# Attention stage: single steps with scores two steps ahead, a fifth slot of probabilities, and another join of the late maxima

## What is computed

```python
def xattn(q, k, v, Wq, Wk, Wv, bv, Wo, bo):       # 16 heads of 32
    qh, kh, vh = heads(q @ Wq.T), heads(k @ Wk.T), heads(v @ Wv.T + bv)
    scores = einsum('bhsd,bhtd->bhst', qh, kh) / sqrt(32)
    mask = triu(ones((S, S)), k=0).at[0, 0].set(False)
    scores = where(mask, -inf, scores)            # strictly causal, query 0 sees key 0
    out = einsum('bhst,bhtd->bhsd', softmax(scores), vh)
    return merge(out) @ Wo.T + bo
x = x + xattn(layernorm(x), ctx, ctx, ...)
x = x + ffn(layernorm(x), controller, f1, bias, f2)   # experts pick tokens by maximum
```

## Time and profile before

| | |
|---|---|
| median of three runs | 1348.98 us (1346.82 to 1352.07) |
| profiled execution | 1353.44 us, span 1351.7 us |
| mean granted TensorE clock over the span | 0.930 |
| busy over the span | PE 89%, PEld 61%, DVE 66%, ACT 45%, POOL 43% |
| attention stage | 313 to 927 us of the span |

### The profile page before, as it was taken

How to read it: one execution, slowest core, us unless ns; L and a number is a source line. 1 busy time by engine, 2 the same in 40 slices (tenths; PEclk the granted TensorE clock), 3 DMA queues, 4 the chain that set the end, 5 groups by cost and what they waited for, 6 DMA issues and landing times. The chain is left out here.

```text
span 1351.7 us, 29427 instructions
## 1 busy us (share of the span) xinstructions
PE 1203.2 (89%) x11456; PEld 830.9 (61%) x11456; DVE 890.0 (66%) x2198; ACT 612.6 (45%) x1143; POOL 583.6 (43%) x799
## 2 busy tenths in 40 slices
PE   5999999976889999999999999993799988898773
PEld 4888888853445555555555555541588877875552
DVE  6555555525666877777777778740578865559994
ACT  3222222201545555556656566552244444366651
POOL 0000000003446767777666666674576734302333
PEclk9999999995999999999999999997799977678986
DMA  6665555549623455555554444203788955453344
GB/s 228 217 217 207 213 210 209 186 156 198 143 68 77 108 126 126 126 126 126 126 125 106 114 113 113 69 17 112 266 260 264 297 168 188 168 190 89 111 128 148
DMA packets 163885, 210.77 MB, mean 156 GB/s; under 512 B 8880, under 2 KB 96560, under 8 KB 162736
## 3 DMA queue, kind: packets, MB, share of 16 engines
q1 hardware_dynamic: 163760, 209.06, 53.3%
HBM read 131.17 MB, written 77.59 MB: 154 GB/s over the span
## 5 line engine op out<-in xcount | busy, mean ns | idle before, releaser
L718 ACT ACTIVATE p_t<-p_bank 128x512 f32<-128x512 f32 (+1 forms) x608 | 310.2, 589 | 222.9 <-PE p_bank L778 217.3
L759 PE MATMUL p_bank<-k_stack,q_stack 96*128 96x512 f32 (+3 forms) x768 | 285.2, 394 | 28.8 <-DMA ident<-in_ident 19.3
L664 DVE CUSTOM_DVE_ANT_0 tried<-p_bank,ban 128x128 bf16<-128x128 f32 (+3 forms) x512 | 236.5, 485 | 86.1 <-PE p_bank L759 86.0
L778 PE MATMUL p_bank<-q_stack,k_stack 97*128 97x512 f32 (+3 forms) x768 | 258.9, 358 | 10.4 <-ACT p_t L718 6.0
L759 PEld LDWEIGHTS p_bank<-k_stack,q_stack 96*128 96x128 f32 x768 | 145.8, 193 | 152.8 <-issue 64.2
L667 DVE TENSOR_REDUCE mx_a<-p_bank 128x1 f32<-128x512 f32 x256 | 175.9, 687 | 62.5 <-PE p_bank L759 61.0
L600 POOL TENSOR_SCALAR_AFFINE_SELECT p_t<-p_t 128x128 f32<-128x128 f32 (+2 forms) x288 | 102.0, 357 | 171.5 <-ACT p_t L718 164.2
L778 PEld LDWEIGHTS p_bank<-q_stack,k_stack 97*128 97x128 f32 x768 | 145.6, 191 | 41.5 <-ACT p_t L718 27.0
L796 PE MATMUL p_bank<-p_t,v_tile 128*32 128x512 f32 (+3 forms) x1536 | 162.9, 497 | 1.6 <-POOL p_t L600 1.2
L611 POOL TENSOR_TENSOR p_sum<-p_sum,p_t 128x512 f32<-128x512 f32 x128 | 159.9, 1281 | 0.5 <-ACT p_t L718 0.5
L584 POOL MEMSET k_stack<- 1x4096 f32 x3 | 10.4, 3506 | 302.3 <-POOLq L128 302.3
(11 more groups left out here) (121 smaller groups left out, 2287.8 us busy)
## 6 DMA issues: line engine op xcount, KB each, us to landing
q_stack<-q_hi SPq DMA_DIRECT2D x64, 256.0 KB, 6.5
k_stack<-k_hi SPq DMA_DIRECT2D x30, 512.0 KB, 9.5
f_sb<-in_f SPq DMA_DIRECT2D x5, 2048.0 KB, 7.9
x_in<-in_x SPq DMA_DIRECT2D x8, 1024.0 KB, 9.1
c_in<-in_ctx_t SPq DMA_DIRECT2D x8, 1024.0 KB, 11.1
k_hi<-k_hi_s SPq DMA_DIRECT2D x8, 1024.0 KB, 4.2
k_lo<-k_lo_s SPq DMA_DIRECT2D x8, 1024.0 KB, 6.4
v_rows<-v_out SPq DMA_DIRECT2D x8, 1024.0 KB, 4.3
```

What stands on the lines that cost most here:

```text
L664: dve.tensor_tensor_reduce(tried[:, TRIED[c]:TRIED[c] + w], got, ban0[:] if i == 0 else ban[:, CH - w:CH], 1.0, -3e38, ALU.add, ALU.max, t ...
L718: act.activation(pt[:, k % SLOTS_P, u * m:(u + 1) * m, 0:w], bank[:, SB + n % SR, 0:m * w].rearrange("p (m w) -> p m w", m=m), ACT.Exp, sc ...
L759: pe.matmul(bank[:, to, 0:w], qs[it % SLOTS][0:R, i * P // CH, h, i * P % CH:i * P % CH + P], ks[it % SLOTS][0:R, h, t0:t0 + w], start=Tru ...
L778: mm = pe.matmul(bank[:, SB + n % SR, h % m * w:(h % m + 1) * w], ks[slot][0:R + 1, h, j * P:(j + 1) * P], qs[slot][0:R + 1, sh, h, CH - w ...
```

## The change

From iteration 3 on the groups are single steps. In step k, `full_width` issues the four scores of step k + 2 (`coming`, with `AHEAD = 2`), with that step's chunks dealt into the four score slots by `portions`, and then the values and sums of step k. Iterations 0 to 2 stay one step ahead, and the last step of iteration 2 issues the scores of two. The plan for iterations 3 on has new lengths (`even`) and weighs VectorE's inversions (`busy`), which now stand before steps 1 and 5. The late turn comes before the chunks of the fourth score slot of step 0 (it was the second of eight). ScalarE takes the second half's results after the first exp of step 2 (it was the third), the first half's after the first exp of step 6 (it was after all of them), and negates the late maxima after the third exp of step 2. `p_t` has five slots, numbered through all iterations by `slot_p`. The buffer `tried` is as long as one of its halves, used again by the late chunks behind a wait. `mx_a` and `mx_b` are one tensor `mx_ab`, and a `tensor_reduce` over its middle axis makes `mx_l`.

```diff
-    TRIED = [sum(c[3] for c in CHUNKS[:n] if c[4]) for n in range(NC + 1)]
+    TRIED = [sum(c[3] for c in CHUNKS[EARLY * (n >= EARLY):n] if c[4]) for n in range(NC)]
+    TRIED_ALL = sum(c[3] for c in CHUNKS[:EARLY])
-    GROUPS = [[[k] for k in range(NS)] if it < SINGLE else [[k, k + 1] for k in range(0, NS, 2)] for it in range(NIT)]
+    AHEAD = 2
-    SPREAD_AT = [None if it < SINGLE else 2 for it in range(NIT)]
-    SLOTS_P = 4
+    SLOTS_P = 5
     def inversions(it):
-        return {2: 1, 7: 0} if it < SINGLE else {1: 1, 3: 0}
+        return {2: 1, 7: 0} if it < SINGLE else {1: 1, 5: 0}
+    def coming(it, k):
+
+        if it < SINGLE:
+            todo = [k + 1] if k + 1 < NS else [NS + i for i in range(AHEAD if it + 1 == SINGLE else 1)]
+        else:
+            todo = [k + AHEAD]
+        return [(it + n // NS, n % NS) for n in todo if it + n // NS < NIT]
+    def portions(chunks, slots):
+
+        out = []
+        for i in range(slots):
+            out.append(-(-(chunks - sum(out)) // (slots - i)))
+        return out
+    LATE_SLOT = 3
...
+        even = [0.85 * SPAN[k][1] / CH * (1 if k in FULL[:-1] else 2) + 0.3 + 4 * max(0.12, SPAN[(k + AHEAD) % NS][1] / 2400)
+                for k in range(NS)]
-            long = [sum(length[k] for k in group) if it < SINGLE else 1.0 for group in GROUPS[it]]
+            long = short if it < SINGLE else even
-            busy = 1.75 if it < SINGLE else 0.0
+            busy = 1.75
...
-        mx_a = sb("mx_a", [P, HG * ST // 2], F32)
-        mx_b = sb("mx_b", [P, HG * ST // 2], F32)
+        mx_ab = sb("mx_ab", [P, 2, HG * ST // 2], F32)
+        def slot_p(it, k):
+            return (it * NS + k) % SLOTS_P
...
-                    if c == EARLY and it > 0:
-                        dve.wait_ge(mx_ready, it)
+                    if c == EARLY:
+                        dve.wait_ge(mx_read, n)
+                        if it > 0:
+                            dve.wait_ge(mx_ready, it)
-                        dve.tensor_tensor(mx_l[:], mx_a[:], mx_b[:], ALU.max).then_inc(mx_ready, 1)
+                        dve.tensor_reduce(mx_l[:], mx_ab[:].rearrange("p t c -> p c t"), AX.X, ALU.max).then_inc(mx_ready, 1)
...
-                                if k == SPREAD_AT[it] and u == 0:
-                                    negate(2 * it + 1)
-                                if k == SPREAD_AT[it] and u == 2:
-                                    take(it - 1, 1)
-                            if k == 0 and 0 < it < SINGLE:
+                            if it >= SINGLE and k == AHEAD and u == 0:
                                 take(it - 1, 1)
-                            if k == 4 + lag:
+                            if it >= SINGLE and k == AHEAD and u == LATE_SLOT - 1:
+                                negate(2 * it + 1)
+                            if it >= SINGLE and k == 4 + AHEAD and u == 0:
                                 take(it, 0)
...
-                    ahead = [(k, h) for k in nxt for h in range(HG)]
-                    n, todo, left = BEFORE[it, g], TAKES[it][g], max(1, len(ahead))
-                    for i in range(left):
-                        if it >= SINGLE and g == TURN_LATE[it] and i == 1:
+                    ahead = [(at, k, h) for at, k in coming(it, g) for h in range(HG)]
+                    n = BEFORE[it, g]
+                    for i, count in enumerate(portions(TAKES[it][g], max(1, len(ahead)))):
+                        if it >= SINGLE and g == TURN_LATE[it] and i == LATE_SLOT:
                             turn(2 * it + 1)
-                        for _ in range(-(-todo // (left - i))):
+                        for _ in range(count):
                             chunk(n)
-                            n, todo = n + 1, todo - 1
+                            n += 1
                         if ahead:
-                            score(at, *ahead[i])
+                            score(*ahead[i])
...
-                    for g, group in enumerate(GROUPS[it]):
-                        full_width(it, g)
-                        for k in group:
-                            values(it, k)
-                            if k not in FULL[:-1]:
-                                sums(it, k)
+                    for k in range(NS):
+                        full_width(it, k)
+                        values(it, k)
+                        if k not in FULL[:-1]:
+                            sums(it, k)
```

More of the change, by code:

```diff
@@ L424, in attend @@
     for it in range(NIT):
-        for g in range(len(GROUPS[it])):
+        for g in range(NS):
             BEFORE[it, g] = total
@@ L443, in attend @@
         ban0 = sb("ban0", [P, P], F32)
-        tried = sb("tried", [P, TRIED[NC]], BF16)
+        tried = sb("tried", [P, TRIED_ALL], BF16)
         ident = sb("ident2", [P, P], F32)
@@ L501, in attend @@
         for it in range(NIT):
-            for g in range(len(GROUPS[it])):
-                first = -(-TAKES[it][g] // (2 * HG))
+            for g in range(NS):
                 if it < SINGLE and g == TURN_LATE[it]:
@@ L507, in attend @@
                     place("turn", 2 * it + 2)
+                first = sum(portions(TAKES[it][g], max(1, HG * len(coming(it, g))))[:LATE_SLOT])
                 for n in range(TAKES[it][g]):
@@ L593, in mask @@
                         if STEPS[k][1] == 0:
-                            pool.tensor_tensor(pt[:, k % SLOTS_P, u, 0:1], e0, e0, ALU.mult)
-                            part = pt[:, k % SLOTS_P, u, 1:P]
+                            pool.tensor_tensor(pt[:, slot_p(it, k), u, 0:1], e0, e0, ALU.mult)
+                            part = pt[:, slot_p(it, k), u, 1:P]
                             pool.affine_select(part, part, [[1, P - 1]], ALU.is_ge, 0.0, base=0,
@@ new lines, in _ @@
+                    for k in range(NS):
+                        w, m = SPAN[k][1], TOGETHER[k]
+                        for u in range(UNITS[k]):
+                            n = it * UNIT0[NS] + UNIT0[k] + u
+                            act.wait_ge(scored, n + 1)
+                            if u == 0 and it * NS + k >= SLOTS_P:
+                                act.wait_ge(step_done, it * NS + k - SLOTS_P + 1)
+                                old = (it * NS + k - SLOTS_P) // NS, (it * NS + k - SLOTS_P) % NS
+                                if old[1] in FULL:
+                                    act.wait_ge(joined, (old[0] * JOINS + max(1, FULL.index(old[1]))) * HG)
+                            act.activation(pt[:, slot_p(it, k), u * m:(u + 1) * m, 0:w],
+                                           bank[:, SB + n % SR, 0:m * w].rearrange("p (m w) -> p m w", m=m), ACT.Exp,
+                                           scale=SCALE).then_inc(exp_done, 1)
+                            if it >= SINGLE and k == AHEAD and u == 0:
@@ L726, in _ @@
                                 take(it - 1, 1)
-                            if k == 4 + lag:
+                            if it >= SINGLE and k == AHEAD and u == LATE_SLOT - 1:
+                                negate(2 * it + 1)
+                            if it >= SINGLE and k == 4 + AHEAD and u == 0:
                                 take(it, 0)
-                        if it < SINGLE and g == TURN_LATE[it]:
-                            negate(2 * it + 1)
-                        if g == TURN_EARLY[it]:
+                        if it < SINGLE:
+                            if k == 0 and it > 0:
+                                take(it - 1, 1)
+                            if k == 4:
+                                take(it, 0)
+                            if k == TURN_LATE[it]:
+                                negate(2 * it + 1)
+                            if k == TURN_EARLY[it]:
+                                negate(2 * it + 2)
+                        elif TURN_EARLY[it] is not None and k == TURN_EARLY[it] + AHEAD - 1:
```

31 lines of the change are left out of this document (8 added, 23 removed).

## The result

The changed kernel takes 1382.4 us in the median of four runs (1379.1 to 1385.4), the kernel before 1350.5 in the runs beside it: ratio 1.0216, 95% interval 1.0183 to 1.0248. It is 2.2% slower, by 32 us. I had forecast slower, but 1364, and my range ended at 1377.

What follows compares the result with a forecast made beforehand. Bound: TensorE's path, with waits at two rings of three PSUM banks, GpSimd's joins right under it. 12 x 1.35 = 16.2, + 0.4, - 1.8 = +14.8 us gave 1363.8, say 1364; forecast 1358 to 1370, range 1341 to 1377.

Steps and rivals of the forecast that it cites:

- Values and sums in twelve blocks, 14.55 us: TensorE, iterations 3 to 14: same matmuls in twelve blocks instead of six, 14.55 us per iteration, 0.85 more.
- Full-width blocks, 22.6 us: TensorE's score and chunk blocks, iterations 3 to 14: twelve blocks sum to 22.6 us per iteration, against 22.2.
- waits: Kernel before, inside full-width blocks: some 4.6 us per iteration waiting at the two rings of three PSUM banks.
- smoothing gives nothing: Full-width blocks: no gain, because chunks come in lumps of six, which a ring of three takes no better than eight.
- The check by iteration 2, 37.9 us: Iteration 2, already in single steps: its 40.35 us, adjusted for extra scores and chunks, would be 37.9.
- GpSimd's chain: GpSimd's joins and masks, 17.44 us, first join 18.3 us after the start: iteration not under 36.8, hidden by TensorE's 37.2.
- smoothing works: Rival: ring waits shrink, GpSimd then sets a period of 35.6 or 35.0 us; kernel 1337 to 1344; chance 0.18.
- The late turn and its DMA: Turn two score slots later, DMA landing at 5.0 to 5.5 us, before its score: cost 0, up to 0.5 if slipped.
- The fifth slot: Probability buffer: removes a wait of exp 9 for join 1, worth 0 to 1.2 us in iterations 0 to 2; taken 0.
- The join of late maxima: VectorE's reduction at 0.2 us: 3 x 0.6 = 1.8 us gained in iterations 0 to 2, 0 in 3 to 14.
- Iteration 15: Last iteration: step 7's exp at 15.1 instead of 14.7 us after its start, the 17.4 us chain following: +0.4.
- lumps cost more: Rival: six-chunk blocks cost what iteration 2 shows (37.9 to 38.2 us): +25 us, 1374; chance 0.23.

Runs made afterwards that it cites:

- all-fast cuts: Changed kernel and kernel before, each with maxima cut to 32 columns, exps to 64, joins to 32: 35.10 and 33.09 us per iteration.
- a_even: Changed kernel with four chunks in every step from iteration 3 on: 36.8 us per iteration; 1363.6 us, ratio to the kernel before 1.0104.
- b_halves_fast_early: Kernel before, maxima, exps and joins cut (32, 64, 32 columns), values between full-width halves, PSUM copies after first exps of steps 2 and 6: 36.4 us per iteration.

## Why the prediction was right in its direction and wrong in its size

By its own steps:

- **Values and sums in twelve blocks, 14.55 us:** 14.56. Right.
- **Full-width blocks, 22.6 us:** 24.0. This step failed: I had them grow by 0.4 us, and they grew by 1.8. I had set a sum of my own prices, 22.6, against a measured 22.2 of the kernel before, and had called the 4.6 us by which the measured figure passed my prices "waits". They were not all waits. By the all-fast cuts the kernel before waits 35.85 - 33.09 = 2.8 us, and its full-width work without waits is 33.09 - 13.7 = 19.4 us, where my prices give 17.5 + 6 x 0.12 = 18.2. In the changed kernel it is 35.10 - 14.55 = 20.55, where they give 17.5 + 12 x 0.12 = 18.9. So the work without waits was priced 1.6 us too low; the waits (3.7 in my sum, 38.5 - 35.1 = 3.4 measured) were 0.3 too high.
- **Where the 1.6 lies:** a block's first full-width matmul holds TensorE 0.10 longer, which I had left out, and its last 0.09 longer, where I had 0.12. Over twelve blocks that is 0.8. The other 0.8 is in both kernels, as the same difference gives it for each (20.55 - 17.5 - 12 x 0.19 and 19.4 - 17.5 - 6 x 0.19, with 0.19 for 0.10 + 0.09): my price by width is too low for narrow matmuls and for wide ones behind them, such as the chunk of 0.28 us above. That none of this is a wait shows in the blocks of steps 3, 7, 8, 9 and 10: 1.77, 2.01, 1.18, 1.89 and 1.95 us in the all-fast cut, within 0.01 of that in the whole kernel, and 1.50, 1.98, 1.05, 1.85 and 1.85 in my sum. Step 3's 1.50 is also a slip: by my own prices it is 0.61 for the chunks, 0.93 for the scores and 0.12, some 1.67.
- **Why "smoothing gives nothing":** for two reasons, and I named one. Lumps cost 1.7 us of the iteration (`a_even`). Changes of kind cost 2.0 (the two all-fast cuts), of which I had 0.14 + 0.12 each, 1.6, spread over two terms. Smoothing does cut waits once the lumps are gone: 36.8 - 35.1 = 1.7 us of waits in the evenly dealt kernel, 2.8 in the paired one, if the even deal without waits takes 35.1 too, which no run shows. It pays 2.0 to save 1.1.
- **The check by iteration 2, 37.9 us:** nearer to 38.5 than my sum. It was a measurement of the same kind of order, and I kept it as a rival with half the chance of my sum's. It should have weighed more, since a block-by-block sum leaves out what isn't known to be there.
- **GpSimd's chain:** predicted first join 18.3 us after the start, found 19.0; bound 36.8, so found 37.4, under TensorE's 38.5. No wait for joins in the changed kernel; with one step of lead it is the bound. Right. The 35.6 us of the rival "smoothing works" is a slip of 0.4: its first term of 15.2, with 1.52 + 17.44 + 1.01, gives 35.2.
- **The late turn and its DMA:** no wait for it in iterations 3 to 15. Right. Why it moved to the fourth slot I had not seen; `b_halves_fast_early` shows it.
- **The fifth slot:** taken at 0, found 0.
- **The join of late maxima:** the time, 0.19 us, was right; the gain of 1.8 us was not there. I took the median of 788 ns over all 16 joins and the three waits of iterations 0 to 2, and never looked whether these were the same joins. They aren't:

```profile
427.88 0.18 DVE L672 TENSOR_TENSOR mx_l<-mx_a,mx_b 128x16 f32<-128x16 f32 x1
```

This is the join of the kernel before in iteration 2; those of iterations 0 and 1 took 0.18 as well. The slow ones come later, where nothing waits for them.

- **Iteration 15:** +0.4 predicted; the attention stage grew by 33.1 us in all, 32.15 between the starts of iterations 3 and 15, -0.2 before and +1.1 behind. The forecast's sum was 14.8 for the same.

The direction was no luck in its main part: of the 2.67 us per iteration, 0.85 in values and sums was forecast and found, and that TensorE pays for the order itself is shown. The +0.4 in the full-width blocks had its sign by chance, as a difference of two figures that do not count the same things. The rival "lumps cost more" (1374) was short as well, by 0.47 us in each of twelve iterations and by the 1.8 us of the late join.

## What to carry over

Count the places where an engine changes the kind of its work, and take the price of one from a stretch without waits, at both its ends and at its first instruction, before giving up large blocks for even ones. Do not compare a sum of prices for the new order with a measured time of the old one. Price both by the same prices first, and see what these leave unexplained in the one that is measured. A stretch of the same kernel that already runs the new order is worth more than a sum of parts. And where a median is applied to particular instructions, look at these instructions.

## What the hardware showed

TensorE's change from values and sums (fp32, four 32-column tiles) to full-width matmuls and back costs 0.10 us at the first full-width matmul, 0.09 at the last and 0.12 at the end of the values, at full clock and with nothing to wait for. Why, the trace doesn't say.

VectorE's tensor_tensor on 16 columns takes 0.18 us three times in iterations 0 to 2, 0.21 at the end of iteration 2, and 0.77 to 0.84 from iteration 3 on. In the kernel before, in iteration 13 (GpSimd, then VectorE), its end falls together with that of a GpSimd mask on 512 columns:

```profile
856.64 0.64 POOL L600 TENSOR_SCALAR_AFFINE_SELECT p_t<-p_t 128x512 f32<-128x512 f32 x1
```

```profile
856.51 0.80 DVE L672 TENSOR_TENSOR mx_l<-mx_a,mx_b 128x16 f32<-128x16 f32 x1
```

With the reduction alone changed (`b_reduce`), the same mask starts 0.05 us behind the join, and the join does not wait for it:

```profile
853.63 0.66 POOL L599 TENSOR_SCALAR_AFFINE_SELECT p_t<-p_t 128x512 f32<-128x512 f32 x1
```

```profile
853.58 0.19 DVE L671 TENSOR_REDUCE mx_l<-mx_ab 128x16 f32<-128x32 f32 x1
```

All sixteen of these joins take 0.185 to 0.188 us. Not every mask has this effect: the tensor_tensor of 427.88 us takes 0.18 us while GpSimd is busy with four masks on 128 columns (427.28 to 428.75). That the join of two tensors is held up and the reduction of one is not agrees with the Trainium skill (GPSIMD Engine Reference, Key points), which says that GpSimd and VectorE contend where a VectorE instruction has two SBUF inputs.
